# Local attention with 64-row matmuls: eight score tiles at a time, row halves in two PSUM banks, and a new order on all five queues

## What is computed

```python
def attn_layer(x, Wqkv, qs, ksc, Wo):          # 16 heads of 64, windows of 32 tokens
    q, k, v = split(x @ Wqkv)                  # 128 -> 3 * 1024
    q, k = rotary(l2norm(q) * qs), rotary(l2norm(k) * ksc)
    # each window of 32 queries sees its own 32 keys and the 32 before them
    sim = einsum('bhwie,bhwje->bhwij', bq, bk2) * 8.0
    attn = softmax(where(mask, -big, sim))
    return einsum('bhwij,bhwje->bhwie', attn, bv2) @ Wo    # 1024 -> 128

for i in range(6):
    x = attn_layer(shift_tokens(x), ...) + x
    x = ffn_layer(shift_tokens(x), ...) + x    # layer norm, 128 -> 2*341, a*gelu(gate), 341 -> 128
```

## Time and profile before

| | us |
|---|---|
| median of 3 runs (4095.67 to 4100.74) | 4097.78 |
| profiled execution, own time | 4098.77 |
| its span, first to last instruction | 4096.9 |
| the six layers in it, first to last matmul of a layer | about 988 to 4064 |

### The profile page before, as it was taken

The page is one execution under the profiler, slowest core; times in us unless marked ns, Lnnn a source line. Parts: engine busy times, 40 slices in busy tenths (PEclk is TensorE's granted clock), DMA queues, the critical chain, the costliest instruction groups (busy, mean ns, idle before and its releaser), DMA issues. The chain is left out here.

```text
span 4096.9 us, 125398 instructions
## 1 busy us (share of the span) xinstructions
PE 3940.0 (96%) x43636; PEld 2914.0 (71%) x43636; DVE 3450.4 (84%) x8234; ACT 3771.9 (92%) x7378; POOL 2329.4 (57%) x2684
## 2 busy tenths in 40 slices
PE   4999999997999999999999999999999999999995
PEld 2566666663777777777777777777777777777774
DVE  4788888875988888888888888888888888888884
ACT  4899999985999999999999999999999999999995
POOL 4000000006777777777777777777777777777773
PEclk7899999997999999999999999999999999999997
DMA  6777777752111111111111111111111111111111
GB/s 180 223 232 231 228 228 230 234 176 75 49 44 47 46 40 44 44 49 46 39 44 49 44 49 35 49 44 49 44 38 46 49 44 44 49 36 48 44 49 54
DMA packets 249745, 347.67 MB, mean 85 GB/s; under 512 B 45104, under 2 KB 206364, under 8 KB 249116
## 3 DMA queue, kind: packets, MB, share of 16 engines
q1 hardware_dynamic: 249244, 340.94, 27.9%
HBM read 151.06 MB, written 82.85 MB: 57 GB/s over the span
## 5 line engine op out<-in xcount | busy, mean ns | idle before, releaser
L1468 PE MATMUL la_ps<-la_Wqkv,la_xsT 128*128 128x512 f32 x2304 | 1172.8, 602 | 6.8 <-DVE X L1164 6.8
L1164 DVE TENSOR_TENSOR X<-la_ps,la_tab 128x1024 f32<-128x1024 f32 x768 | 938.2, 1222 | 102.0 <-ACT la_sq L1312 95.6
L1094 POOL TENSOR_TENSOR la_rt<-X 128x512 f32<-128x512 f32 x384 | 495.9, 1291 | 589.9 <-PE la_ps L1483 436.6
L1111 POOL TENSOR_TENSOR la_rt<-la_rt,la_rn 128x1024 f32<-128x1024 f32 x384 | 722.4, 1902 | 27.5
L1173 DVE TENSOR_REDUCE la_ssum<-la_sq 128x8 f32<-128x512 f32 x768 | 511.1, 666 | 0.0
L1312 ACT ACTIVATE la_sq<-la_ps 128x512 f32<-128x512 f32 x768 | 464.9, 605 | 34.8 <-PE la_ps L1468 30.1
L1095 POOL TENSOR_TENSOR la_rt<-X 128x512 f32<-128x512 f32 x384 | 495.6, 1291 | 0.0
L527 POOL COPY at_vh<-V 128x64 f32 (+1 forms) x64 | 15.1, 236 | 783.9 <-PE at_ps L726 782.7
L1499 PEld LDWEIGHTS la_ps<-la_kT,la_qB 128*64 128x64 f32 x12288 | 390.4, 138 | 85.1 <-issue 73.7
L1468 PEld LDWEIGHTS la_ps<-la_Wqkv,la_xsT 128*128 128x128 f32 x2304 | 362.3, 190 | 120.3 <-issue 75.3
L1499 PE MATMUL la_ps<-la_kT,la_qB 128*64 128x64 f32 x12288 | 432.9, 224 | 0.0
(11 more groups left out here) (204 smaller groups left out, 9046.2 us busy)
## 6 DMA issues: line engine op xcount, KB each, us to landing
at_band<-skew_scratch SPq DMA_DIRECT2D x64, 1536.0 KB, 7.3
la_vs<-la_v SPq DMA_DIRECT2D x192, 384.0 KB, 3.5
skew_scratch<-at_R SPq DMA_DIRECT2D x64, 1024.0 KB, 6.7
la_vs<-la_v SPq DMA_DIRECT2D x192, 128.0 KB, 3.4
la_Wqkv<-in_wqkv SPq DMA_DIRECT2D x28, 384.0 KB, 5.4
at_qh<-qt_scratch SPq DMA_DIRECT2D x64, 144.0 KB
at_kh<-kt_scratch SPq DMA_DIRECT2D x64, 144.0 KB
la_W<-in_L_ffn_W SPq DMA_DIRECT2D x24, 341.0 KB, 5.2
```

The lines of the kernel that those rows point to most:

```text
L1094: e.tensor_tensor(dst[:, :, 0, :], c[:, :, 0, :], s[:, :, 1, :], ALU.add)
L1111: e.tensor_tensor(heads(rt, w), heads(rt, w), wide(rn[:, w * H:(w + 1) * H], D), ALU.mult)\
L1164: e.tensor_tensor(dst.rearrange("p f (h d) -> p f h d", d=D), ps[:, c % 2, :].rearrange("p (h d) -> p h d", d=D).unsqueeze(1).to_broadcast ...
L1468: e.matmul(ps[:, c % 2, :], xsT[:, m * P:(m + 1) * P], Wqkv[:, ds(layer(n) % 2, 1), c * 512:(c + 1) * 512], start=True, stop=True)\
```

## The change

Scores and values get 64 rows for each matmul. `qB` becomes `qT` and `pB` becomes `pT`, plain turned copies without zeros. A matmul of scores takes the 64 rows of one head (`of`), 32 stationary columns (a window's queries) and 64 moving columns; the head of rows 0 to 63 writes bank 2, the other bank 3 (`BANK_S + par`), and eight in a row address eight different places of the array (two row halves by four column groups of 32). There are 64 of them for a tile. A matmul of values takes 64 rows (`wl`, one pair of windows), 64 stationary and 32 moving columns, with the row halves in banks 4 and 5; there are 64 of them too. Scores and values are no longer cut into halves: both wait for all of their inputs and report once. ScalarE's `q_turned` and `p_turned` are one 128x512 copy for each half instead of two 64x512. `table_of` loads a ScalarE table when the last one loaded in program order was another, and stands in `guess`, `exp` and `gelu`.

```diff
-DEEPEST = 7
+DEEPEST = 8
-        TURNED_Q, TURNED_K, TURNED_P, OUT = (4, 5), (5, 4), (5, 4), (5, 4)
-        N_IN, SET = 7, 7
+        TURNED_Q, TURNED_K, TURNED_P, OUT = (4, 5), (5, 4), (5, 4), (4, 5)
+        N_IN, SET = 7, 6
...
+            loaded = []
+
+            def table_of(name):
+                if loaded[-1:] != [name]:
+                    e.preload_act_table_set(name)
+                    loaded.append(name)
...
             def q_turned(n, m, u):
-
-                src = ps[:, TURNED_Q[u], :].rearrange("p (j w q) -> p j w q", j=4, w=WPT)
                 e.wait_ge(Tq_mm.sem, Tq_mm.v(n, u + 1))
-                e.wait_ge(S_mm.sem, S_mm.v(n - 1, u + 1))
-                e.activation(qB[0:D, 4 * u:4 * u + 4, :, 0, :], src[0:D], ACT.Copy)
-                e.activation(qB[D:P, 4 * u:4 * u + 4, :, 1, :], src[D:P], ACT.Copy).then_inc(Tq_ev.sem, 1)
+                e.wait_ge(S_mm.sem, S_mm.v(n - 1))
+                e.activation(qT[:, 4 * u:4 * u + 4, :], ps[:, TURNED_Q[u], :].rearrange("p (j t) -> p j t", j=4),
+                             ACT.Copy).then_inc(Tq_ev.sem, 1)
...
-            def scores(n, m, h):
...
-                bank = ps[:, BANK_S + h, :]
-                for j in range(4):
+            def scores(n, m):
...
+                for c in range(4):
                     for wl in range(2):
-                        for g in range(2):
-                            w, col = g + 2 * wl, j * P + wl * D
-                            at = m % RING_V * P + w * WIN
-                            mm = e.matmul(bank[g * D:(g + 1) * D, col:col + D], qB[:, 4 * h + j, w, :, :],
-                                          kT[:, 4 * h + j, at:at + 2 * WIN], start=False, stop=True,
-                                          skip_group_check=True)
-                mm.then_inc(S_mm.sem, 1)
+                        for jj in range(2):
+                            for g in range(2):
+                                w, at = g + 2 * wl, m % RING_V * P + (g + 2 * wl) * WIN
+                                to = slice((2 * g + jj) * WIN, (2 * g + jj + 1) * WIN)
+                                col = c * P + wl * D
+                                for par in range(2):
+                                    of = slice(par * D, (par + 1) * D)
+                                    mm = e.matmul(ps[to, BANK_S + par, col:col + D], qT[of, 2 * c + jj, w * WIN:(w + 1) * WIN],
+                                                  kT[of, 2 * c + jj, at:at + 2 * WIN], start=False, stop=True,
+                                                  skip_group_check=True)
+                mm.then_inc(S_mm.sem, 2)
...
-                for j in range(4):
-                    pair = 4 * h + j
+                for pair in range(H // 2):
+                    c, jj = pair // 2, pair % 2
                     for g in range(2):
+                        keys = (vs[:, m % 2, :], v[:, m % RING_V, :])[g]
+                        at, to = (2 * g + jj) * WIN, pair * D + g * WIN
                         for par in range(2):
-                            keys = (vs[:, m % 2, :], v[:, m % RING_V, :])[g]
                             head, rows = (2 * pair + par) * D, slice(par * D, (par + 1) * D)
-                            to = ps[rows, OUT[h], j * P:(j + 1) * P].rearrange("p (l g q) -> p l g q", l=2, g=2)
-                            mm = e.matmul(to[:, :, g, :], keys[:, head:head + D], pB[:, pair, 2 * g + par, :, :],
-                                          start=True, stop=True, skip_group_check=True)
-                mm.then_inc(pv_mm.sem, 1)
+                            for wl in range(2):
+                                of = slice(wl * D, (wl + 1) * D)
+                                mm = e.matmul(ps[rows, OUT[wl], to:to + WIN], keys[of, head:head + D],
+                                              pT[of, 4 * par + c, at:at + WIN], start=True, stop=True, skip_group_check=True)
+                mm.then_inc(pv_mm.sem, 2)
```

More of the change, by code:

```diff
@@ L1279, in body @@
                         gated(n, m, 1)
+                for n, m in t.back(2):
+                    largest(n, m, 0)
+                    largest(n, m, 1)
+                    below(n, m, 0)
                 for n, m in t.back(0):
-                    turned(n, m, 0)
-                    squares(n, m, 0)
-                for n, m in t.back(6):
-                    if m % 2:
-                        next_x(n, m)
-                for n, m in t.back(5):
-                    if m % 2:
-                        gated(n, m, 2)
-                for n, m in t.back(0):
-                    turned(n, m, 1)
-                for n, m in t.back(4):
-                    stats(n, m)
+                    squares(n, m, 1)
             straight(e, body, TILES, TB, DEEPEST)
@@ L1388, in body @@
             def body(t):
[L1389 to L1393 removed]
+                for n, m in t.back(5):
+                    k_turned(n, m, 1)
+                for n, m in t.back(3):
+                    squared(n, m, 0)
+                for n, m in t.back(5):
+                    masked(n, m, 0)
+                    masked(n, m, 1)
+                for n, m in t.back(3):
+                    squared(n, m, 1)
@@ new lines, in body @@
+                for n, m in t.back(6):
+                    p_turned(n, m, 0)
+                    p_turned(n, m, 1)
+                for n, m in t.back(7):
+                    one(n, m)
+                for n, m in t.back(8):
+                    if m % 2:
+                        gelu(n, m, 1)
+                for n, m in t.back(4):
+                    guess(n, m)
+                for n, m in t.back(6):
+                    o_out(n, m, 0)
+                for n, m in t.back(7):
+                    y_turned(n, m)
@@ L1394, in body @@
+                for n, m in t.back(6):
+                    o_out(n, m, 1)
+                for n, m in t.back(3):
+                    squared(n, m, 2)
+                for n, m in t.back(5):
+                    exp(n, m, 0)
+                for n, m in t.back(3):
+                    squared(n, m, 3)
+                for n, m in t.back(5):
+                    exp(n, m, 1)
                 for n, m in t.back(7):
                     if m % 2:
+                        gelu(n, m, 0)
+                for n, m in t.back(8):
+                    if m % 2:
@@ L1410, in body @@
-                for n, m in t.back(5):
-                    o_out(n, m, 0)
+                for n, m in t.back(4):
+                    q_turned(n, m, 0)
+                    q_turned(n, m, 1)
+                for n, m in t.back(3):
+                    v_out(n, m, 4)
                 for n, m in t.back(0):
                     x_turned(n, m)
-                for n, m in t.back(6):
-                    one(n, m)
+                for n, m in t.back(3):
+                    v_out(n, m, 5)
                 for n, m in t.back(4):
-                    exp(n, m, 0)
@@ L1627, in body @@
                         hidden(n, m, 0)
+                for n, m in t.back(7):
+                    if m % 2:
+                        hidden(n, m, 2)
                 for n, m in t.back(5):
```

233 lines of the change are left out of this document (91 added, 142 removed).

## The result

The changed kernel takes 4471.38 us (median, 4455.23 to 4479.06), the kernel before 4098.67: a ratio of 1.0905, 95% interval 1.0872 to 1.0937. The forecast was 4026, in a range of 3900 to 4160; it is 373 us slower where 73 less were forecast.

What follows compares the result with a forecast made beforehand. TensorE was taken as the bound at 15.83 us a tile. Scores and values fall from 3.88 to 3.48 us (1.3 + 0.15 + 0.08 + 1.88 + 0.12, less 0.05), so 4099 - 192 x 0.40 + 5 = 4027, median 4026; range 3900 to 4160.

Steps and rivals of the forecast that it cites:

- second limit of term 1: TensorE's queue feed in scores: 0.016 us a record, so 128 records take 2.0 us, as an upper end.
- Term 1, scores after: TensorE's scores block: 128 records at eight places side by side, between 0.94 and 2.0 us, taken as 1.3 a tile.
- Row halves take turns: Scores and values: row halves do not run side by side, scores 1.88 and values 3.76 us, total 4500; 16 in 100.
- Term 2, the seam: Between scores and values on TensorE: exposed waits 0.15 us a tile, plus 0.08 for one more change of array shape.
- Term 3, values after: TensorE's values block: weight loads keep a record at 0.059 us, so 1.88 us a tile, no gain; bounds 0.94 and 2.8.
- Values gain too: Values at 1.4 us or less, block 3.0 or less, VectorE takes over at 14.6 to 14.9: 3885 to 3925; 10 in 100.
- ScalarE: 14.3 forecast: ScalarE's busy time a tile: 15.39 less 2.4 for shorter copies plus 1.28 for more table loads, below TensorE's 15.43.
- the milder rival by the tables: Table loads hold ScalarE as long again before they begin: ScalarE 15.6 us a tile, total 4066; 1 in 100.
- The new order counted as nothing: All engines' new order keeps TensorE full, with slacks of 0.2 to 1.8 us, so it costs 0.
- the edges at +5: End of the layers: lag of 8 adds one iteration, taken as 5 us in all, bounds 0 and 13.5.
- If the covers go: New order failing to hide other engines' work from TensorE: 0.4 us a tile lost, the whole gain.
- One record per 0.029 us at best: TensorE record starts limited to 0.029 us apart: 256 records take 7.5 us, total 4810; 7 in 100.

Runs made afterwards that it cites:

- half: The changed kernel with every second scores matmul group and every second values pair left out, so half the attention is not computed: 3798.29 us, ratio 0.9271.
- order_single: Kernel before with the new engine orders, old 128-row matmuls, q_turned and p_turned copying each half once flat (not the attention's values): 4099.12 us, ratio 0.9997.
- weave_b: The changed kernel with scores and values each cut in two parts and other TensorE work between, next_x one place later: 4498.59 us, ratio 1.0978.

## Why the prediction was wrong

**The step that failed is the second limit of term 1**, "how fast PE's queue is fed". It took one short stretch in which 32 records left the queue at 0.016 us each and made a rate of it for 128. The short rate was right, even low: 128 in 1.27 us. What no step asked is whether 512 instructions in place of 256 can be brought in at that rate, block of 256 after block. They can't; that cost 1.58 us a tile in gaps and some 0.35 behind them. With 0.34 of seams (15.77 against the 15.43 forecast) these are the 2.28 us a tile between forecast and result. The sum had no term for the supply, and none of the rivals did. The page of before showed the queue that does it, q8 with 321 packets, and I passed it over at its share of 0.6%. Its share says nothing: what counts is the time over 256 instructions in the densest place.

**Term 1, scores after:** 1.3 forecast, 1.27 measured. Row halves do run side by side, which refutes the rival *Row halves take turns*: by it scores could not take less than 1.88, and eight records wouldn't start within a tenth of a microsecond while each is shown as lasting 0.24. The records of scores in the window 3025.7 to 3025.9 (durations, first and last start):

```profile
L1495 PE MATMUL la_ps<-la_kT,la_qT x8: 240/240/240, 3025.8 to 3025.9; 64*32 64x64 f32 x8
```

The rival's 4500 us lay nearest to the result by accident; its sizes, 1.88 for scores and 3.76 for values, aren't there.

**Term 2, the seam:** 0.15 + 0.08, with the 0.12 of before; measured 0.46 between scores and values, five waits in PE's queue 0.11 apart where I took 0.05, and some 0.15 more into `turn_y`. It was mis-sized by about 0.3. It alone would have eaten most of the gain: half makes the block without gaps 3.82 us against 3.92 in order_single.

**Term 3, values after:** 1.88 forecast, 1.86 measured without the gaps. The rival *Values gain too* is out. (Its lower end was worked out wrongly: a tile of 14.6 us gives 4099 - 192 x 1.23 + 5 = 3868, not 3885. Nothing here hangs on it.)

**ScalarE:** 14.3 forecast; 1624.63 of 2000 us of a 17.71 us tile are 14.4. The four table loads a pair are there, and the next instruction starts 1.29 us after the load began, so the milder rival by the tables is out as well:

```profile
3027.34 1.28 ACT L1317 ACT_TABLE_LOAD   x1
3028.63 0.23 ACT L1324 ACTIVATE la_lns<-la_hs 128x32 f32<-128x32 f32 x1
```

**The new order counted as nothing, the edges at +5:** both right, by order_single, whose period is that of before while its end, from the last `turn_x` on, is 5.1 us longer. "If the covers go" was sized at 0.4 a tile; with the old copies they did go, and it was 1.3.

**One record per 0.029 us at best:** out. Records of scores start 0.007 us apart at first and 0.011 over the rest of a block. By the Trainium skill (TensorE: Matmul & The Clock Gate, "Wait — 56ns, not 53.3ns?") starts never come closer than about 25 ns; eight places fed in turn are well below it here.

What stays open: what makes a packet start, which came at times more than 4 us after the queue had entered the block before, and so how dense 256 instructions may be. Kernels with 3.57 us or more had no gaps, weave_b with 2.41 us had 16, and half, with 1.98 us, only two; no threshold was measured. That the lower clock accounts for all of the 0.35 behind the gaps was only argued.

## What to carry to other kernels

Cutting matmuls into more and smaller ones has a price that no engine's share shows: find the densest place, take the time over 256 queue records there, and where it falls well below what the kernel ran at before, expect gaps that no semaphore explains. Read "issue" in front of PE as a question about its instructions, count the distance between gaps, and set the packets of the instruction queue beside them. When an order made for shorter copies is judged, judge it with the short copies; a part of a change taken alone can lose for a reason that the whole does not have.

## What the runs showed of the hardware

- Records with 64 rows and 32 columns of weights, at eight places, start 0.010 us apart on the mean of 128 (1.27 us); with 64 rows and 64 columns, at four places, 0.0145. Each has its own weight load.
- A wait that is already met costs PE's queue 0.11 us when it stands between short matmuls (five in 0.53 us).
- A record of 128 rows, 64 columns of weights and 16 moving columns takes 0.033 us, one of 64 moving columns 0.029: cutting by columns in four made the kernel 61% slower.
- PE's instructions came in packets of 16.4 KB, one for each 256 queue records, 0.9 to 1.4 us long ahead of a gap in the changed kernel, and no block of 256 began sooner than 1.19 us after its packet's end.
- Where the packet was late PE stood still: 124 gaps of 0.6 to 2.4 us in 2000 us, at exact multiples of 256 records. After some of the longer ones the granted clock was 0.50, in 102 of the 2000 us.
